# All twelve portions of neighbour rows split into high and low parts, with their 0/1 tables made piece by piece

## Time and profile before

| what | us |
|---|---|
| median of 3 runs (lowest, highest) | 2996.17 (2993.83, 2996.44) |
| the profiled execution, its span | 2996.88, 2995.4 |
| key stage and start of the loop | about 605 to 857 |
| one iteration of the loop | 87.6 |

### The profile page before, as it was taken

How to read it: one execution, slowest core, us unless ns; L and a number is a source line. 1 busy time by engine, 2 the same in 40 slices (tenths; PEclk the granted TensorE clock), 3 DMA queues, 4 the chain that set the end, 5 groups by cost and what they waited for, 6 DMA issues and landing times.

```text
span 2995.4 us, 47258 instructions
## 1 busy us (share of the span) xinstructions
PE 2914.0 (97%) x16707; PEld 2561.0 (85%) x16708; DVE 2190.0 (73%) x5317; ACT 1762.9 (59%) x3392; POOL 1674.2 (56%) x1700
## 2 busy tenths in 40 slices
PE   7999999979989999999999999999999999999998
PEld 5887878868878888888888988888988888888887
DVE  5489564145677887777788777778887777888775
ACT  4455555524456666665666666566665666666554
POOL 1000000052267777777777777777777777777750
PEclk9999999989999999999999999999999999999999
DMA  7777777765444434444443444444344444434430
GB/s 275 272 264 274 265 275 288 293 214 199 145 130 127 128 109 133 134 130 134 122 130 106 129 130 132 133 122 126 114 134 134 134 124 130 121 121 134 134 85 11
DMA packets 181936, 471.35 MB, mean 157 GB/s; under 512 B 46902, under 2 KB 105228, under 8 KB 159715
## 3 DMA queue, kind: packets, MB, share of 16 engines
q0 software_dynamic: 80544, 221.54, 25.6%
q1 hardware_dynamic: 98960, 244.93, 22.6%
q10 hardware_dynamic: 2196, 1.86, 0.2%
HBM read 310.71 MB, written 158.29 MB: 157 GB/s over the span
## 4 chain that ended last, share of the span: by engine, by line
PE 63%; POOL 6%; DVE 5%; issue 3%; ACT 1%; DVEq 1%; DMA 0%; SPq 0%; ACTq 0%; POOLq 0%
PE bank L1670 41%; PE acc L1727 7%; PE acc L1733 7%; POOL ring L1150 6%; PE acc L1670 2%; DVE sel L1381 2%; PE bank L1834 1%; PE bank L1697 1%; DVE x L1480 1%; PE bank L1706 1%; PE bank L1716 1%; DVE h_lo L1510 1%; DVE stats_c L1484 1%; PE bank L1783 1%; DVEq L1482 1%
## 5 line engine op out<-in xcount | busy, mean ns | idle before, releaser
L1150 POOL DMA_INDIRECT ring<-y_tab,tab x1666 | 1657.5, 995 | 633.8 <-issue 499.7
L1224 ACT ACTIVATE h_hi<-bank,bias_t 128x512 fp32r<-128x512 f32 (+1 forms) x600 | 407.3, 679 | 302.1 <-PE bank L1670 268.5
L1510 DVE TENSOR_TENSOR h_lo<-bank,h_hi 128x512 fp32r<-128x512 f32 (+1 forms) x600 | 382.0, 674 | 229.8 <-ACT bank L1225 227.8
L778 PE MATMUL yb<-wr_hi,xhl 128*128 128x512 f32 x1568 | 498.2, 394 | 13.1 <-ACT yst L355 11.1
L1210 ACT ACTIVATE row_hi<-ring,tab 128x256 fp32r<-128x256 f32 x1091 | 451.7, 498 | 33.3 <-issue 17.7
L1401 DVE SCALAR_TENSOR_TENSOR row_lo<-ring,tab,row_hi 128x256 fp32r<-128x256 f32 x1091 | 449.4, 478 | 9.4 <-ACT row_hi L1210 9.2
L1225 ACT ACTIVATE bank<-bank,bias_t 128x512 f32<-128x512 f32 (+1 forms) x600 | 386.3, 644 | 0.0
L355 ACT ACTIVATE yst<-yb 128x512 f32<-128x512 f32 x392 | 229.3, 596 | 249.4 <-PE yb L778 219.1
L778 PEld LDWEIGHTS yb<-wr_hi,xhl 128*128 128x128 f32 x1568 | 296.2, 189 | 79.9 <-ACT yst L355 15.8
L1670 PE MATMUL bank<-ew_hi,h_hi 128*128 128x256 f32 x1176 | 343.5, 292 | 1.6 <-DVE h_lo L1510 1.4
L1670 PE MATMUL bank<-ew_lo,h_hi 128*128 128x256 f32 x1176 | 330.8, 281 | 0.0
(11 more groups left out here) (265 smaller groups left out, 5506.6 us busy)
## 6 DMA issues: line engine op xcount, KB each, us to landing
y_tab<-yst SPq DMA_DIRECT2D x97, 1024.0 KB, 4.4
ring<-y_tab,tab POOLq DMA_INDIRECT x1666, 2.8
xt_tab<-xhl SPq DMA_DIRECT2D x25, 1024.0 KB, 4.8
xc<-xt_tab SPq DMA_DIRECT2D x25, 1024.0 KB, 5.5
xhl<-xt_tab SPq DMA_DIRECT2D x23, 1024.0 KB, 5.0
x<-x_tab SPq DMA_DIRECT2D x49, 256.0 KB, 3.1
xs<-in_x SPq DMA_DIRECT2D x24, 512.0 KB, 6.0
x_tab<-xs SPq DMA_DIRECT2D x24, 512.0 KB, 5.1
```

What stands on the lines that cost most here:

```text
L778: last = pe.matmul(out_ap, a, b, start=(i == 0), stop=(i == len(parts) - 1))
L1150: pool.indirect_dma_start(out=out_ap, out_offset=None, in_=y_tab[:, :], in_offset=bass.IndirectOffsetOnAxis(ap=idx_ap, axis=0)).then_inc(s ...
L1224: act.activation(dest[:, m, 0:W], b[:, 0:W], ACT.Relu, bias=bias)
L1510: gone(dve.tensor_tensor(lo_[:, m, 0:W], bank[plan[kind, (e, m)][0]][:, 0:W], hi[:, m, 0:W].bitcast(F32), ALU.subtract))
```

## The change

- `PLAIN` is 0: portions 0 to 3 are split too, so all 68 tiles take the way of the second bullet above.
- VectorE's two functions for a split portion become one, `split`: for each tile one 128-wide 0/1 table and then that tile's low rows, after the wait for ScalarE's high rows.
- ScalarE gets the high rows of portions 0 to 3. Those of the super-tile after next stand at e = 4 (portion 0) and e = 5 (portion 1), those of portions 2 and 3 after the layer-normed transposes and after the first layer of expert 0.
- ScalarE makes `rel_w` (`tables`, four small activations with a table of negative tile starts), and spreads the attention's reciprocals over 32 columns each (`by_feature`), both of which VectorE did.
- VectorE makes portion 0 of the super-tile after next at the end of e = 4, portion 1 in e = 5, and portion 2 behind the low half of the transposed features rather than ahead of it.

```diff
-PLAIN = 4
+PLAIN = 0
+NEXT_AT = {4: 0, 5: 1}
...
+                def by_feature(i):
+                    act.wait_ge(rden_set, i + 2)
+                    act.activation(rden_c[:, :, :].rearrange("p t (h d) -> p (t h) d", h=HEADS),
+                                   rden[:, :, :].rearrange("p t h -> p (t h)").unsqueeze(2)
+                                   .to_broadcast([P, SUB * HEADS, C // HEADS]), ACT.Copy).then_inc(rden_ready, 1)
+
+                def tables(n):
+                    act.wait_ge(tab_in[n % 2], 16 * SUB * (n // 2 + 1))
+                    for t in range(SUB):
+                        last = act.activation(rel_w[:, n % 2, t, :], tab[:, n % 2, t, :, 1], ACT.Identity,
+                                              bias=neg_t[:, SUB * n + t:SUB * n + t + 1])
+                    last.then_inc(rel_set, 1)
...
+                    if more:
+                        high(i + 1, 2)
                     b = take(i, plan, "rh", 0)
                     gone(act.activation(rh[:, 0:W], b[:, 0:W], ACT.Relu, bias=bias_t[:, RB1:RB1 + 1]))
                     for m in range(KC):
                         hidden("h1", 0, m)
+                    if more:
+                        high(i + 1, 3)
...
+                        if more and e == 1:
+                            by_feature(i)
                         for p in SPLIT_AT.get(e, ()) if more else ():
                             high(i + 1, p)
+                        if e in NEXT_AT and i + 2 < SUPER:
+                            high(i + 2, NEXT_AT[e])
+                        if more and e == EXPERTS - 3 and i + 2 < SUPER:
+                            tables(i + 2)
...
-                    dve.reciprocal(rden[:, :, :], rden[:, :, :])
-                    dve.drain()
-                    dve.tensor_copy(rden_c[:, :, :].rearrange("p t (h d) -> p (t h) d", h=HEADS),
-                                    rden[:, :, :].rearrange("p t h -> p (t h)").unsqueeze(2)
-                                    .to_broadcast([P, SUB * HEADS, C // HEADS])).then_inc(rden_ready, 1)
+                    dve.reciprocal(rden[:, :, :], rden[:, :, :]).then_inc(rden_set, 1)
...
+                def split(n, p):
+                    if p >= parts(n):
+                        return
+                    tables_free(dve, n, p)
+                    if p == 0:
+                        dve.wait_ge(rel_set, n + 1)
+                    dve.wait_ge(hi_ready, split_before(n, p) + 1)
+                    for q, (t, k) in enumerate(tiles_of_portion(p)):
+                        dve.tensor_tensor(hot_r[:, p % BUFS, q:q + 1, :], ramp[:, 0:NT].unsqueeze(1).to_broadcast([P, 1, NT]),
+                                          rel_w[:, n % 2, t, k:k + 1].unsqueeze(2).to_broadcast([P, 1, NT]), ALU.is_equal)
+                        last = dve.scalar_tensor_tensor(out=row_lo[:, p % SLOTS, q, :], in0=ring[:, p % SLOTS, q, :],
+                                                        scalar=tab[:, n % 2, t, k, 2:3],
+                                                        in1=row_hi[:, p % BUFS, q, :].bitcast(F32),
+                                                        op0=ALU.mult, op1=ALU.subtract)
+                    last.then_inc(lo_ready, 1)
...
-                        for p in coming:
-                            one_hot(i + 1, p)
                         if e == EXPERTS - 1 and i + 2 < SUPER:
-                            prepare(i + 2, 0)
-                            prepare(i + 2, 1)
+                            prepare(i + 2, NEXT_AT[e])
...
                             if h == 0 and coming:
-                                low_rows(i + 1, coming[0])
+                                split(i + 1, coming[0])
...
                         for p in coming[1:]:
-                            low_rows(i + 1, p)
-                        if more and e == EXPERTS - 3:
-                            if i + 2 < SUPER:
-                                tables(i + 2)
+                            split(i + 1, p)
+                        if e == EXPERTS - 2 and i + 2 < SUPER:
+                            prepare(i + 2, NEXT_AT[e])
```

More of the change, by code:

```diff
@@ L911, in gps_layer @@
             base_t = sbuf(pc, "base_t", [P, TILES_N])
+            neg_t = sbuf(pc, "neg_t", [P, TROWS])
             xtab = sbuf(pc, "xtab", [P, 3])
@@ L978, in gps_layer @@
             emptied = {"act": sem("act_emptied"), "dve": sem("dve_emptied")}
-            rden_ready, acc_full, x1_done = (sem(n) for n in ("rden_ready", "acc_full", "x1_done"))
+            rden_set, rel_set, rden_ready, acc_full, x1_done = (sem(n) for n in ("rden_set", "rel_set", "rden_ready", "acc_full", "x1_done"))
             var_c, std_c, xn_c, d_ready, ex_ready, gap_ready, g2_ready, gate_ready = (
@@ L1143, in _ @@
                           allow_small_or_imprecise_dtypes=True).then_inc(base_set, 1)
+                pool.iota(neg_t[:, :], pattern=[[-NT, TROWS]], base=0, channel_multiplier=0,
+                          allow_small_or_imprecise_dtypes=True).then_inc(neg_set, 1)
                 def count(register):
@@ L1271, in key_parts @@
                     act.activation(kf[:, v % 2, :].rearrange("p (k n) -> p k n", k=KC), z, ACT.Relu).then_inc(key_e, 1)
+                act.wait_ge(neg_set, 1)
+                tables(0)
+                tables(1)
                 for p in range(PARTS):
@@ L1289, in _ @@
                         gone(act.activation(kw_sb[:, :, :], b[:, :].rearrange("p (k n) -> p k n", k=KC), ACT.Copy))
+                        by_feature(-1)
                     if p in WEIGHTS_AT:
@@ L1295, in _ @@
                         act.activation(w_hi[j][:, :, :, :], stage[j % 2][:, :, :, :], ACT.Copy).then_inc(w_hi_set, 1)
+                high(1, 0)
+                high(1, 1)
                 for s in range(SUPER - 1):
@@ L1366, in attention @@
                         gone(dve.tensor_tensor(qf[:, k, :], qf[:, k, :], b[:, 0:NS], ALU.mult))
[L1368 to L1374, removed]
                 def weighted(n, p):
@@ L1378, in weighted @@
                         return
+                    dve.wait_ge(rel_set, n + 1)
                     tables_free(dve, n, p)
                     for q, (t, k) in enumerate(tiles_of_portion(p)):
-                        last = dve.tensor_scalar(sel[:, p % BUFS, q, :], iota_w[:, :], rel_w[:, n % 2, t, k:k + 1],
+                        last = dve.tensor_scalar(sel[:, p % BUFS, q, :], ramp[:, 0:NT], rel_w[:, n % 2, t, k:k + 1],
                                                  tab[:, n % 2, t, k, 2:3], ALU.is_equal, ALU.mult)
@@ L1411, in prepare @@
                     else:
-                        one_hot(n, p)
-                        low_rows(n, p)
+                        split(n, p)
                 def by_expert(v, n):
@@ L1515, in iteration @@
                         query_features(i, plan)
-                        prepare(i + 1, 2)
                     dve.wait_ge(items_full, full(i, plan, "ft", KC - 1))
@@ L1521, in iteration @@
                                                ft_hi[:, k, 0:W].bitcast(F32), ALU.subtract))
+                    if more:
+                        prepare(i + 1, 2)
                     low("h1", 0)
@@ L1596, in _ @@
                 dve.memset(zv[:, :, :, :], 1.0)
-                tables(0)
+                dve.drain()
                 for p in range(PARTS):
@@ L1627, in _ @@
                                           ALU.subtract).then_inc(w_split_c, 1)
-                tables(1)
                 prepare(1, 0)
```

4 lines of the change are left out of this document (2 added, 2 removed).

## The result

The changed kernel takes 3205.8 us (median of four runs, 3198.4 to 3211.1), the one before 2995.0 on the same chip: a ratio of 1.070, 95% interval 1.068 to 1.073. The forecast was 3140 with a range of 2998 to 3220. The time lies near the upper end of that range. The profiled execution took 3211.1 us around a span of 3209.6.

What follows compares the result with a forecast made beforehand. PE paced the loop at 87.60 us, with gathers also without room; after the change VectorE's chain would take 93.6 us per round. 2996.9 + 138 over 23 rounds + 5 at the ends gave 3140 us, range 2998 to 3220.

Steps and rivals of the forecast that it cites:

- A single table: VectorE's 0/1 table for one tile: 0.195 us of pace, between 0.135 and 0.257; near 0.27 by its own length.
- PE's 83.0: PE's work per iteration after the change, in us: 4.0 less, because portions 0 to 3 are split.
- The chain: VectorE's strictly ordered work and its waits for PE and ScalarE, in five stretches: 93.6 us per round, 6.0 more.
- The fifth step: From portion 5 to the next round's first y of expert 5: 51.5 us busy plus 1.8 idle, 53.3.
- stretch 4: From expert 0's second y through denominators, gates, spread and portion 5's high rows, which VectorE waits for: 7.7 us.
- steps 1 and 4: Second query projection up to the features' low half, 7.3 us; denominators up to portion 5's high rows, 7.7 us.
- The waits named: PE waiting for VectorE: second query projection 3.7 us, denominators 1.5, expert 3's first layer 2, portions 6 and 10 under 1.
- The last full iteration: PE gains 4.0 us but loses about 3 at the query projection and 5 in experts 0 and 1: +4.
- The key stage: PE gets up to 4 us back, ScalarE's tables ahead of the first key tile may take as much: +1.
- PE's gain: Rival: PE's 4.0 us per iteration come through, 24 x 4.0 = 96 us, giving 2901; chance 0.09.
- The gather stream: Rival: GpSimd's gathers, 87.9 us per super-tile, stay the bound and VectorE keeps up; about 3000 us; chance 0.13.
- what I had argued for `sel`: Beside gathers, `sel` should by the two-port rule be a worse neighbour than low rows, so removing it would help.

Runs made afterwards that it cites:

- early_and_root: Changed kernel with the root product moved ahead of the second query projection and work around the denominators reordered to free their bank early; 3028.7 us.
- root_twice: Changed kernel with the root's 24 matmuls also done once ahead of the second query projection, only to keep PE busy; 3173.1 us.
- bank_early: Changed kernel with VectorE, PE and ScalarE work reordered around the denominators so that their bank is free earlier; 3128.6 us.
- whole_tables: Changed kernel with one 0/1 table per whole portion ahead of its low rows, in place of one per tile; 3110.3 us.
- four_plain: Changed kernel with portions 0 to 3 plain (not split) again, the rest of the change kept; 3102.0 us.
- two_plain_late: early_and_root with portions 7 and 10 plain, and portions 0 to 3 of the first super-tile plain; single tables kept; 3062.0 us.
- triples: early_and_root with 0/1 tables in pieces of three tiles, and portions 0 to 3 plain in the first super-tile only; 2989.9 us.
- no_low_rows: triples without making or summing low rows from the second super-tile on, so the output is incomplete; 2926.8 us.

## Why the prediction was right or wrong

**Prices.** Right. A single table takes 0.282 us by its own row (0.275 forecast) and a tile 0.59 (0.591). VectorE is busy for 79.4 us (79.9), ScalarE for 67.0 (65 to 70), the spread takes 1.04 (1.05). PE's 83.0 came out some 2 us low: at full clock it is busy for 84.49 in 88 us of a round of 88.7 (early_and_root).

**The chain.** Right: without the drops of the clock, its five stretches are 7.18 (root_twice), 9.58, 15.9, 7.65 (rounds of the changed kernel without a drop there) and 53.3, together 93.6. The fifth step, which I trusted least, was off by nothing, in part by luck: 50.9 us busy where I had 51.5, and 2.3 idle where I kept 1.8. The order of events in stretch 4 was not quite mine: VectorE's long wait is ahead of the first y of expert 1 (4.06 us), which PE delivers late, and only 0.44 is left ahead of portion 5.

**The terms that were mis-sized** are steps 1 and 4. I priced PE's work on the path (4.37, 4.35) by rows at full clock, and at the same time wrote that PE would stand still just ahead of it for 3.7 and 1.5 us. PE did (3.39, 1.67), and then ran at half clock: 7.3 became 8.9 and 7.7 became 8.8, 2.7 us per round. Over 23 rounds that is 62 of the 66 us by which 204 exceeds 138. For the first step root_twice shows that the wait is the cause. For the fourth, rounds of one kernel with a drop (8.1 to 10.4) and without (7.65) show its price, but not what brings it on: bank_early took the wait ahead of the denominators away and still has a drop in 7 of 22 rounds, whole_tables kept a wait of 1.0 to 1.5 us and has one in 22, and before has the same group of matmuls, without a wait ahead and without a drop. That stays open. That the time lies inside the range is luck: its upper part was there for the price of a single table, which was right, and no term of it stood for the clock.

**The waits named.** PE waits 3.39 us at the second query projection (3.7 forecast), 1.4 at the denominators (27.3 over 19; 1.5), under 1 elsewhere, at the first layer of expert 3 too, where I had 2. In the round shown PE is idle for 8.1 us (some ten forecast).

**The ends.** The last full iteration was +4.3 (+4 forecast). The key stage cost 7.4, not 1. The split explains little of it: in the five versions whose first super-tile has its portions 0 to 3 plain (four_plain, and those from two_plain_late to triples) the first low half starts at 872.8 to 879.4 us, against 874.3 in the changed kernel and 866.9 before. What the other edits cost there, one by one, no run shows.

**The rivals.** PE's gain didn't come through, for the reason given. The gather stream was no bound of the changed kernel, since GpSimd waits; but it is the floor beneath every version, at 85.1 us without hold-ups and 87 to 89 with them, and before already stood on it. So a PE that needs 83 us has next to nothing to win here, even with the chain mended (5 us in triples). Of the gathers' neighbours I looked at the wrong one: `sel` lengthens them by 0.01 us, the low rows by 0.14 (the counts at no_low_rows). The Trainium skill (SBUF — State Buffer, "SBUF: two separate sides") names two kinds of VectorE instruction that hold the port shared with GpSimd: those in a two-port mode, from which I argued for `sel`, and those with two SBUF inputs, against a GpSimd instruction that reads SBUF. The low row has two (the ring and its high row), and a gather takes its row numbers from the edge table in SBUF. The counts fit the second kind, and not what I had argued for `sel`. That the port is the mechanism is my reading of the Trainium skill; the runs show only which instruction it is.

## What to carry to other kernels

When engines of 70 to 90% load hand work to each other in strict order, add up the path once round, not the loads; at full clock each stretch here came out to a few tenths. Into a wait of TensorE put work that doesn't need the answer (the root): here it shortened the path and kept the clock up, 4.3 us for 8.9. And before relieving an engine, check what else has no slack: here the gathers, at 87.9 of 87.6 us, would have taken back nearly all of any gain.

## What the runs showed of the hardware

TensorE's granted clock fell to 0.5 inside a loop that keeps the engine busy for 88 of 96 us: beside a wait of 3.39 us, and after a wait of 1.67 with sixteen four-column matmuls behind it, for 3.4 or 6.8 us each by the records. It cost 2.7 us per round. Behind the same sixteen matmuls it fell in 7 of 22 rounds without that wait (bank_early), and in one of 22 with a wait of 1.0 to 1.5 us (whole_tables). With 24 matmuls of no use in the first wait it stayed at 1.00 there. A gather of 128 rows takes GpSimd 0.946 us and 0.305 of issue without low rows (no_low_rows), and up to 3.26 beside a run of them (before; 2.40 in the earlier trace rows).
